# Mixture-of-experts gate: lane tables on POOL, and a running sum along the tiles for the tokens' ranks

## The chip, the core and the metric

The kernel runs on one core of a Trainium2 chip. The core has PE (matrix products, results in PSUM), DVE (elementwise work and reductions), ACT (activation functions), POOL (a second, programmable elementwise engine, which also issues the indirect gathers) and SP, whose queue issues plain transfers. The engines run side by side and wait for each other through semaphores. The metric is the device time of one execution in microseconds. Three timed executions of the kernel before stand beside one profiled execution.

## What is computed

The program is two layers of a graph network over 6250 nodes with 256 features. Each layer has a sum over 100,000 edges and an attention part; the first is followed by a mixture of experts, the second by a feed-forward part on selected nodes. The change lies in the gate of the mixture of experts:

```python
gate_logits = x @ gate_w + gate_b                    # 6250 x 16 experts
topk_vals, topk_idx = jax.lax.top_k(gate_logits, K)  # K = 2
topk_w = jax.nn.softmax(topk_vals, axis=-1)
h = jax.nn.relu(jnp.einsum('bsh,ehf->bsef', x, w1) + b1)
expert_out = jnp.einsum('bsef,efh->bseh', h, w2) + b2
sel = jnp.take_along_axis(expert_out, topk_idx[:, :, :, None], axis=2)
moe = jnp.sum(topk_w[..., None] * sel, axis=2)
```

The kernel computes each expert only for the tokens that chose it. The gate therefore has to give each of the two choices of every token a place: the rank of the token among all tokens of that expert, and a start for the expert.

## The kernel before

Each token is a partition in one of T = 49 tiles of P = 128 tokens. The gate, `gate()` from line 1281, works in C = 7 chunks of CT = 7 tiles. It has no planner; every engine's order is written out by hand, and a `wait_ge` on a counting semaphore stands ahead of whatever needs another's result.

**ACT** per chunk: the root of the variance (`root`, L1380), then per tile the normalisation (`apply`, L1384) and a copy of the transposed tile out of PSUM (`copy_xxt`, L1389).

**PE** per chunk c: first `rank(c - 2)`, then per tile two transposes (`turn`, L1639) and two products with the gate's weights (`gate`, L1647). `rank` counts, for each token of chunk c, the tokens ahead of it that chose the same expert. `taken[:, c, 0:CT, :]` is 1 where a token picked an expert. A strictly triangular matrix `before` counts the partitions ahead within a tile (L1654), six products with `ones` add the earlier tiles of the chunk (L1656, with 96, 80, 64, 48, 32 and 16 columns), and one adds everything up to the chunk's start, held in slot CT of `taken` (L1657). After the last chunk one product sums the experts' totals (`column_ps`, L1672), 24 filler products keep PE busy (`busy`, L1278), and 98 products build the list of slots from tables and masks (L1683).

**DVE** is a software pipeline over the chunks. While chunk c is normalised (`sums` L1419, `moments` L1425, `scales` L1430 and L1432), chunk c - 2 is chosen (`bias`, `best`, `equal`, `weigh`, `first`, `choose`, `leave_out`, the middle four twice, then `take` L1477 and `carry` L1483), chunk c - 3 gets its lanes and windows from the ranks (`own` L1489, `rank` L1494, `to_whole` to `window_number`), and for chunk c - 4 `mark` makes the 14 lane tables (L1524). A table is a row of 128 numbers a token that holds the tile's number at the token's lane and zero elsewhere. `mark` stands in seven pairs among the others. `take` comes ahead of `scales(c)`, `carry` behind it.

Behind the loop, a chain of small instructions turns the totals into the experts' offsets (L1591 to L1608, each `link` waits for itself); between its steps stand the work of the last chunk and the seven pairs of `mark(C - 2)`. Then come seven wide comparisons (`high`, L1612), each followed by a scaling on DVE (L1617) or on ACT (L1403); the 14 tables of the last chunk follow the third of them. POOL has no work in the gate.

Of the kernel before, what the change touches and what calls it, by code (L numbers as in the profile page):

```python
# [247 lines left out]
class Kernel:  # L248
# [1031 lines left out]
    def gate(self):  # L1280
# [10 lines left out]
        with ExitStack() as ctx:  # L1291
# [18 lines left out]
            taken = s.sb("taken", [P, C + 1, CT + 1, E], BF16)  # L1310
            ones = s.sb("ones", [P, P], BF16)
            before = s.sb("before", [P, P], BF16)
            own_rank = s.sb("own_rank", [P, 2, CT, E])
# [36 lines left out]
            CH = 14  # L1350
            PL = 7
            by_act = [c for c in range(C - 1) if c % 2]
# [5 lines left out]
            with nc.Block() as block:  # L1358
                @block.sync
                def _(sp):  # L1360
# [13 lines left out]
                    sp.wait_ge(self.beta_in, 16)  # L1374

# [30 lines left out]
                def _(dve):  # L1406
                    n = [0]

                    def link(ins, j=None):
                        ins.then_inc(chain, 1)  # L1410
                        n[0] += 1
                        if j is not None:
                            mark(C - 2, j)
                        dve.wait_ge(chain, n[0])
# [59 lines left out]
                    def take(c):  # L1474
                        if 0 <= c < C:
                            dve.wait_ge(chosen, CH * c + 12)
                            nc.vector.tensor_tensor(taken[:, c, 0:CT, :], pick[:, c, 0, :, :], pick[:, c, 1, :, :], ALU.add).then_inc(chosen, 1)  # L1477

                    def carry(c):
                        if 0 <= c < C:  # L1480
                            dve.wait_ge(chosen, CH * c + 13)
                            with nc.allow_low_precision(reason="whole numbers up to T"):
                                nc.vector.tensor_reduce(taken[:, c + 1, CT, :], taken[:, c, :, :].rearrange("p t e -> p e t"), AX_X, ALU.add).then_inc(chosen, 1)  # L1483
# [44 lines left out]
                    nc.vector.memset(taken[:, 0, CT, :], 0.0).then_inc(ready, 1)  # L1528
                    nc.vector.memset(self.listed[:, :], 0).then_inc(ready, 1)
                    nc.vector.tensor_copy(ones[:, :], self.ones[:, :]).then_inc(ready, 1)  # L1530
                    nc.vector.tensor_copy(before[:, :], self.before[:, :]).then_inc(ready, 1)
                    for j in range(CT):
# [8 lines left out]
                    dve.wait_ge(ready, 8)  # L1541
# [1349 lines left out]
```

## Time and profile before

| | us |
|---|---|
| timed runs, median (lowest to highest) | 2626.71 (2626.49 to 2627.77) |
| the profiled execution's own time | 2623.84 |
| its span in the trace | 2622.1 |
| gate, first DVE instruction to the experts' first POOL instruction | 1156.55 to 1259.65 |
| six of seven chunks' scales ready | 1216.61 |
| last chunk's totals ready | 1233.78 |
| first wide comparison | 1240.51 |
| last list product | 1255.55 |

Over the whole span PE is busy 86%, DVE 55%, ACT 33% and POOL 61%. The gate is 103 us of it. A line of the time order gives the start, the length, the engine, the line of the kernel, the operation and what it writes and reads; in brackets stands the idle time before it and what ended it. Lengths of neighbours on one engine overlap, so what an instruction costs is the distance to the next start.

### The profile page before, as it was taken

To read this page: it belongs to the slowest core of one execution; us is meant where nothing else is said; L and a number is where in the kernel's file an instruction comes from. 1 tells how busy PE (TensorE), PEld (TensorE's weight loads), DVE (VectorE), ACT (ScalarE), POOL (GpSimd) and SP (SyncE) were. 2 spreads that over 40 slices of the span, in tenths; PEclk is the share of its full clock that TensorE was granted. 3 is DMA by queue.
4 is the path that set the end of the run, shared out by engine and by line. 5 is a ranking of instruction groups with operands and counts; after the bars stand their busy time and mean duration, and the time that the engine had idled before them with its cause. 6 is when DMAs were issued, how large, how long until landed. Compare 5 with 4: busy or idle time off the path is not lost. (4 is left out here: it accounts for less than half of the span.)

```text
span 2622.1 us, 48474 instructions
## 1 busy us (share of the span) xinstructions
PE 2249.8 (86%) x13041; PEld 1893.4 (72%) x13042; DVE 1438.6 (55%) x3979; ACT 859.8 (33%) x2513; POOL 1596.1 (61%) x2187
## 2 busy tenths in 40 slices
PE   7967777788878766668899999999989999995998
PEld 5745555566656544457799999788879999994898
DVE  9865444445544544458322222478867777777111
ACT  2512222222222111135233333366643434331333
POOL 4777777777777777730465555588855555550333
PEclk9988998878887777655999999999999999997999
DMA  5233333333333333332233343232211111111121
GB/s 165 89 111 103 100 102 100 102 102 101 102 102 102 102 102 102 103 121 71 93 108 106 125 140 108 73 103 78 78 57 43 46 43 44 42 46 55 35 36 29
DMA packets 138623, 227.41 MB, mean 87 GB/s; under 512 B 26651, under 2 KB 99056, under 8 KB 138546
## 3 DMA queue, kind: packets, MB, share of 16 engines
q0 software_dynamic: 56240, 142.70, 19.4%
q1 hardware_dynamic: 81186, 82.10, 9.4%
q10 hardware_dynamic: 1120, 1.71, 0.2%
q8 instruction: 34, 0.56, 0.1%
q14 instruction: 43, 0.35, 0.0%
HBM read 175.10 MB, written 51.30 MB: 86 GB/s over the span
## 5 line engine op out<-in xcount | busy, mean ns | idle before, releaser
L945 POOL DMA_INDIRECT all_XN<-h_table,l_srcI x782 | 770.5, 985 | 243.7 <-issue 231.6
L1148 PE MATMUL gcn_acc<-all_XN,gcn_hot 128*128 128x256 f32 x796 | 258.6, 481 | 131.3 <-DMA all_XN<-h_table,l_srcI 118.5
L1148 PE MATMUL gcn_acc<-all_XN 128*128 128x256 f32 x768 | 247.5, 478 | 112.3 <-DMA all_XN<-h_table,l_srcI 98.2
L1148 PEld LDWEIGHTS gcn_acc<-all_XN,gcn_hot 128*128 128x128 f32 x796 | 180.1, 237 | 193.8 <-issue 123.1
L1148 PEld LDWEIGHTS gcn_acc<-all_XN 128*128 128x128 f32 x768 | 172.1, 235 | 170.2 <-issue 98.1
L1839 ACT ACTIVATE moe_hidden<-moe_hid_ps,moe_b 128x128 f32<-128x128 f32 x420 | 131.6, 364 | 281.4 <-PE moe_hid_ps L1920 281.4
L1920 PEld LDWEIGHTS moe_hid_ps<-moe_xst,held_held 128*128 128x128 f32 x1680 | 203.9, 193 | 11.7 <-issue 7.0
L1045 DVE COPY_PREDICATED gcn_last_seen<-gcn_seen_sb,gcn_seen 128x392 f32<-128x392 int32 x98 | 57.7, 588 | 281.3 <-ACT gcn_seen_sb L879 281.3
L879 ACT COPY gcn_seen_sb<-gcn_seen 128x392 f32<-128x392 f32 x98 | 47.6, 486 | 496.9 <-PE gcn_seen L1155 495.0
L1920 PE MATMUL moe_hid_ps<-moe_xst,held_held 128*128 128x128 f32 x1680 | 207.1, 277 | 1.9 <-DVE moe_xst L1860 1.9
L1927 PE MATMUL moe_y_ps<-held_held,moe_hidden 128*128 128x256 f32 x840 | 199.2, 380 | 0.2 <-DVE moe_y L1891 0.2
L2507 PEld LDWEIGHTS att_hid_ps<-att_xpt,held_held 128*128 128x128 f32 x1568 | 184.2, 193 | 3.3 <-ACT att_xpt L2371 0.7
L2507 PE MATMUL att_hid_ps<-att_xpt,held_held 128*128 128x128 f32 x1568 | 184.4, 276 | 0.5 <-ACT att_xpt L2371 0.5
L2515 PE MATMUL att_f_ps<-held_held 128*128 128x256 f32 x784 | 179.5, 382 | 2.4 <-ACT held_held L2381 1.0
L1037 DVE SCALAR_TENSOR_TENSOR all_X<-gcn_acc,all_XN,all_X 128x256 f32 x392 | 170.1, 474 | 13.3 <-PE gcn_acc L1148 13.1
L1927 PEld LDWEIGHTS moe_y_ps<-held_held,moe_hidden 128*128 128x128 f32 x840 | 151.4, 190 | 17.2 <-issue 0.5
L2515 PEld LDWEIGHTS att_f_ps<-held_held 128*128 128x128 f32 x784 | 145.1, 190 | 24.0 <-ACT held_held L2381 6.0
L1756 POOL DMA_INDIRECT moe_ring<-rows_table,moe_row x108 | 105.9, 980 | 84.0 <-POOL moe_row L1754 78.5
L1860 DVE COPY moe_xst<-moe_turned 128x256 f32<-128x256 f32 x106 | 45.0, 424 | 149.4 <-PE moe_turned L1900 149.4
L2048 POOL DMA_INDIRECT held_held<-slots_out,all_slot x98 | 102.3, 1044 | 35.9 <-issue 16.5
L1754 POOL COPY moe_row<-moe_listed 128x1 int32 (+1 forms) x108 | 21.0, 194 | 158.9 <-POOLq L1265 113.3
L2381 ACT ACTIVATE held_held<-att_hid_ps,early_b 128x128 f32<-128x128 f32 x392 | 110.6, 365 | 18.3 <-PE att_hid_ps L2507 18.3
(431 smaller groups left out, 4702.9 us busy)
## 6 DMA issues: line engine op xcount, KB each, us to landing
held_held<-in_e_w SPq DMA_DIRECT2D x32, 512.0 KB, 4.6
slots_out<-moe_y SPq DMA_DIRECT2D x105, 128.0 KB
all_XN<-h_table,l_srcI POOLq DMA_INDIRECT x782, 2.8
all_X<-in_x SPq DMA_DIRECT2D x7, 896.0 KB, 11.0
rows_table<-all_XN SPq DMA_DIRECT2D x7, 896.0 KB, 4.2
z_table<-held_held SPq DMA_DIRECT2D x49, 128.0 KB, 2.0
x_table<-all_XN SPq DMA_DIRECT2D x49, 128.0 KB, 1.7
out<-all_X SPq DMA_DIRECT2D x49, 128.0 KB
```

The lines of the kernel that those rows point to most:

```text
L945: nc.gpsimd.indirect_dma_start(msg[b][:, c, :], None, self.h_table, bass.IndirectOffsetOnAxis(self.srcI[:, GE * g + c:GE * g + c + 1], 0)) ...
L1037: nc.vector.scalar_tensor_tensor(x, acc[b % NA][:, :], scale[:, k, ds(g, 1)], x, ALU.mult, ALU.add).then_inc(added, 1)
L1045: nc.vector.copy_predicated(last_seen[:, :], seen_sb[k % 2][:, :], seen[k % NP][:, :]).then_inc(lasts_kept, 1)
L1148: last = nc.tensor.matmul(acc[b % NA][:, :], hot[b % NH][:, c, :], msg[b][:, c, :], start=(c == 0), stop=(c == n - 1))
L1756: nc.gpsimd.indirect_dma_start(ring[:, k * D:k * D + D], None, self.rows_table, bass.IndirectOffsetOnAxis(row_1[k][:, :], 0)).then_inc(lan ...
L1839: last = nc.scalar.activation(hidden[:, 2 * k + f, :], hid_ps[k][:, f, :], ACT.Relu, bias=b1[:, c:c + 1])
L1920: last = nc.tensor.matmul(hid_ps[k][:, f, :], w1[p][:, q, c:c + P], xst[:, q, :], start=(q == 0), stop=(q == KB - 1))
L1927: last = nc.tensor.matmul(y_ps[:, :], hidden[:, f, :], w2[p][:, f, :], start=(f == 0), stop=(f == FB0 - 1))
L2048: nc.gpsimd.indirect_dma_start(ys[t % 2][:, c, :], None, self.slots_out, bass.IndirectOffsetOnAxis(self.slot[:, t, c:c + 1], 0)).then_inc( ...
L2381: last = nc.scalar.activation(hidden[:, c, :], hid_ps[k][:, f, :], ACT.Relu, bias=b1[:, c:c + 1])
L2507: last = nc.tensor.matmul(hid_ps[k][:, f, :], W1[:, b, c:c + P], xpt[:, b, :], start=(b == 0), stop=(b == KB - 1))
L2515: last = nc.tensor.matmul(f_ps[:, :], hidden[:, f, :], W2[:, f, :], start=(f == 0), stop=(f == FB1 - 1))
```

## The change

In `gate()` the lane tables leave DVE. A new block on POOL waits for the constants, then chunk by chunk for the lanes (`placed`), and makes the 14 tables with the same operation. All seven chunks are one straight run of 98 instructions.

`taken` is replaced by `upto`, laid out by expert with CT + 1 slots each. `take` writes a chunk's picks into slots 1 to CT (now with a stride); `carry` runs one scan along the 128 numbers, with a multiplier `joined` of zero at each expert's slot 0 and one elsewhere, so that slot j holds the count up to tile j - 1 of the chunk. A new step `carry_on` copies slot CT to the next chunk's slot 0. PE's `rank` is then two products: `before` with slots 1 to CT, and `from_here` = 1 - `before` with slots 0 to CT - 1. It waits for the scan (`chosen` at CH * c + 14) where it waited for `take`. Three more constants are made at the start of the gate.

```diff
+                @block.gpsimd
+                def _(pool):
+                    pool.wait_ge(ready, READY)
+                    for c in range(C):
+                        pool.wait_ge(placed, PL * c + 6)
+                        for j in range(CT):
+                            for i in (j, CT + j):
+                                last = nc.gpsimd.tensor_scalar(tables[:, c, i, :], iota_b[:, :], lane[:, c, i:i + 1], float(CT * c + j + 1), ALU.is_equal, ALU.mult)
+                            last.then_inc(mark_ready, 1)
...
-                            nc.vector.tensor_tensor(taken[:, c, 0:CT, :], pick[:, c, 0, :, :], pick[:, c, 1, :, :], ALU.add).then_inc(chosen, 1)
+                            nc.vector.tensor_tensor(upto[:, c, :, 1:CT + 1].rearrange("p e t -> p t e"), pick[:, c, 0, :, :], pick[:, c, 1, :, :], ALU.add).then_inc(chosen, 1)
...
-                                nc.vector.tensor_reduce(taken[:, c + 1, CT, :], taken[:, c, :, :].rearrange("p t e -> p e t"), AX_X, ALU.add).then_inc(chosen, 1)
+                                nc.vector.tensor_tensor_scan(counts, joined[:, :, :].rearrange("p e t -> p (e t)"), counts, 0.0, ALU.mult, ALU.add).then_inc(chosen, 1)
+
+                    def carry_on(c):
+                        if 0 <= c < C - 1:
+                            dve.wait_ge(chosen, CH * c + 14)
+                            nc.vector.tensor_copy(upto[:, c + 1, :, 0:1], upto[:, c, :, CT:CT + 1]).then_inc(chosen, 1)
...
-                    def mark(c, j):
-                        if 0 <= c < C:
-                            dve.wait_ge(placed, PL * c + 6)
-                            for i in range(j, PC, CT):
-                                last = nc.vector.tensor_scalar(tables[:, c, i, :], iota_b[:, :], lane[:, c, i:i + 1], float(CT * c + j + 1), ALU.is_equal, ALU.mult)
-                            last.then_inc(mark_ready, 1)
...
                     def rank(c):
-                        pe.wait_ge(chosen, CH * c + 13)
+                        pe.wait_ge(chosen, CH * c + 14)
                         after(pe, placed, PL * (c - 2) + 1)
                         ranks = rank_ps[c % 2]
-                        nc.tensor.matmul(ranks[:, :, :], before[:, :], taken[:, c, 0:CT, :], start=True, stop=False)
-                        for later in range(1, CT):
-                            nc.tensor.matmul(ranks[:, later:CT, :], ones[:, :], taken[:, c, 0:CT - later, :], start=False, stop=False)
-                        nc.tensor.matmul(ranks[:, :, :], ones[:, :], taken[:, c, CT:CT + 1, :].broadcast_to([P, CT, E]), start=False, stop=True).then_inc(ranked, 1)
+                        nc.tensor.matmul(ranks[:, :, :], before[:, :], upto[:, c, :, 1:CT + 1].rearrange("p e t -> p t e"), start=True, stop=False)
+                        nc.tensor.matmul(ranks[:, :, :], from_here[:, :], upto[:, c, :, 0:CT].rearrange("p e t -> p t e"), start=False, stop=True).then_inc(ranked, 1)
```

PE's order where chunk 2 begins, before (`gate_logit_ps` are the logits, `gate_turned` the transposes, `gate_rank_ps` the ranks):

```order
L1647 MATMUL gate_logit_ps<-gate_gate_w,gate_xxt 128x16 x4
L1654 MATMUL gate_rank_ps<-gate_taken,gate_before 128x112
L1656 MATMUL gate_rank_ps<-gate_taken,gate_ones 128x96
L1656 MATMUL gate_rank_ps<-gate_taken,gate_ones 128x80
L1656 MATMUL gate_rank_ps<-gate_taken,gate_ones 128x64
L1656 MATMUL gate_rank_ps<-gate_taken,gate_ones 128x48
L1656 MATMUL gate_rank_ps<-gate_taken,gate_ones 128x32
L1656 MATMUL gate_rank_ps<-gate_taken,gate_ones 128x16
L1657 MATMUL gate_rank_ps<-gate_taken,gate_ones 128x112
L1639 MATMUL gate_turned<-all_ident,all_XN 128x128 x4
```

and in the changed kernel:

```order
L1651 MATMUL gate_logit_ps<-gate_gate_w,gate_xxt 128x16 x4
L1658 MATMUL gate_rank_ps<-gate_upto,gate_before 128x112
L1659 MATMUL gate_rank_ps<-gate_upto,gate_from_here 128x112
L1643 MATMUL gate_turned<-all_ident,all_XN 128x128 x4
L1651 MATMUL gate_logit_ps<-gate_gate_w,gate_xxt 128x16 x2
```

Eight products have become two, in the same place between the chunks.

DVE's order in the chain of offsets behind the loop, before (`all_XT` written from `gate_iota_b` is a pair of lane tables, `gate_own_rank` to `gate_window` the last chunk's work):

```order
L1591 TENSOR_SCALAR gate_total_i<-gate_column_ps 128x16
L1524 TENSOR_SCALAR all_XT<-gate_iota_b,gate_lane 128x128 x2
L1489 TENSOR_TENSOR gate_own_rank<-gate_pick,gate_rank_ps 128x224
L1593 TENSOR_SCALAR gate_tiles_i<-gate_total_i 128x16
L1524 TENSOR_SCALAR all_XT<-gate_iota_b,gate_lane 128x128 x2
L1494 TENSOR_REDUCE moe_rank_of<-gate_own_rank 128x14
L1595 TENSOR_SCALAR gate_tiles<-gate_tiles_i 128x16
L1524 TENSOR_SCALAR all_XT<-gate_iota_b,gate_lane 128x128 x2
L1499 CAST gate_whole<-moe_rank_of 128x14
L1597 SCALAR_TENSOR_TENSOR gate_tile_end<-gate_tiles,gate_zero 128x16
```

and in the changed kernel:

```order
L1598 TENSOR_SCALAR gate_total_i<-gate_column_ps 128x16
L1506 TENSOR_TENSOR gate_own_rank<-gate_pick,gate_rank_ps 128x224
L1600 TENSOR_SCALAR gate_tiles_i<-gate_total_i 128x16
L1511 TENSOR_REDUCE moe_rank_of<-gate_own_rank 128x14
L1602 TENSOR_SCALAR gate_tiles<-gate_tiles_i 128x16
L1516 CAST gate_whole<-moe_rank_of 128x14
L1604 SCALAR_TENSOR_TENSOR gate_tile_end<-gate_tiles,gate_zero 128x16
```

The pairs of tables are gone from between the links of the chain; the rest keeps its order.

## Rows read from the trace of the kernel before

**Rows 1.** Busy us by engine in 10 us: PE, PEld, DVE, ACT, POOL; then PE clock.

```profile
1200.00:1210.00 10.00, 9.88 (x55) 9.13 (x54) 9.72 (x56) 6.88 (x18) 0.00 (x0) 0.50 0.27 93
```

**Rows 2.** Time order of DVE (start us, us, line): the chunks' scales.

```profile
1178.68 0.17 DVE L1432 SCALAR_TENSOR_TENSOR gate_shift<-gate_mv,gate_rs 128x7 f32<-128x7 f32 x1
...
1187.81 0.17 DVE L1432 SCALAR_TENSOR_TENSOR gate_shift<-gate_mv,gate_rs 128x7 f32<-128x7 f32 x1
...
1216.38 0.20 DVE L1430 RECIPROCAL gate_rs<-gate_sd 128x7 f32<-128x7 f32 x1 [0.21 <-ACT gate_sd L1380]
1216.61 0.17 DVE L1432 SCALAR_TENSOR_TENSOR gate_shift<-gate_mv,gate_rs 128x7 f32<-128x7 f32 x1
```

**Rows 3.** Time order of ACT and PE where a chunk begins.

```profile
1178.88 1.09 ACT L1384 ACTIVATE all_XN<-all_X,gate_shift,gate_rs 128x256 f32<-128x256 f32 x2 [0.47 <-DVE gate_shift L1432]
1178.94 0.29 PEld L1654 LDWEIGHTS gate_rank_ps<-gate_taken,gate_before 128*128 128x128 bf16 x1
...
1179.54 0.29 PEld L1639 LDWEIGHTS gate_turned<-all_ident,all_XN 128*128 128x128 f32 x2
```

**Rows 4.** Groups by line and shape in the gate: count | busy us, mean ns.

```profile
L1524 DVE TENSOR_SCALAR all_XT<-gate_iota_b,gate_lane 128x128 bf16<-128x128 bf16 x98 | 19.5, 246 | 0.0
...
L1597 DVE TENSOR_TENSOR_SCAN gate_tile_end<-gate_tiles,gate_zero 128x16 f32<-128x16 f32 x1 | 0.2, 180 | 0.0
...
L1600 DVE TENSOR_TENSOR gate_tile_start<-gate_tile_end,gate_tiles 128x16 f32<-128x16 f32 x1 | 0.2, 164 | 0.0
```

**Rows 5.** Time order of DVE while the last chunk is chosen.

```profile
1226.90 0.39 DVE L1489 TENSOR_TENSOR gate_own_rank<-gate_pick,gate_rank_ps 128x224 f32<-128x224 bf16 x1 [0.20 <-PE gate_rank_ps L1657]
...
1231.54 0.41 DVE L1524 TENSOR_SCALAR all_XT<-gate_iota_b,gate_lane 128x128 bf16<-128x128 bf16 x2
1231.86 0.27 DVE L1457 TENSOR_TENSOR gate_marked<-gate_marked,gate_early 128x112 f32<-128x112 f32 x1
1232.16 0.27 DVE L1462 TENSOR_REDUCE gate_number<-gate_marked 128x7 f32<-128x112 f32 x1
...
1233.02 0.38 DVE L1483 TENSOR_REDUCE gate_taken<-gate_taken 128x16 bf16<-128x128 bf16 x1
```

**Rows 6.** Time order: the totals' product and DVE's chain of offsets.

```profile
1233.50 0.22 PE L1672 MATMUL gate_column_ps<-gate_taken,gate_ones 128*128 128x16 bf16 x1
...
1233.78 0.17 DVE L1591 TENSOR_SCALAR gate_total_i<-gate_column_ps 128x16 int32<-128x16 f32 x1 [0.26 <-PE gate_column_ps L1672]
...
1237.20 0.96 DVE L1604 TENSOR_TENSOR held_held<-gate_pick,gate_start_b 128x1568 bf16<-128x1568 bf16 x1
...
1240.51 0.99 DVE L1612 TENSOR_TENSOR all_XT<-gate_tile_of,gate_iota 128x1596 bf16<-128x1596 bf16 x1
```

**Rows 7.** Time order: PE's filler, the last chunk's tables, the list's last products.

```profile
1233.57 8.00 PE L1278 MATMUL gate_list_ps<-all_ones 128*128 128x512 bf16 x24
...
1244.67 2.35 DVE L1524 TENSOR_SCALAR all_XT<-gate_iota_b,gate_lane 128x128 bf16<-128x128 bf16 x14
...
1251.14 4.41 PE L1683 MATMUL gate_list_ps<-all_XT 128*128 128x228 bf16 x42
```

**Rows 8.** Single lines on POOL in other stages: ns min/median/max.

```profile
L473 POOL TENSOR_SCALAR front_shift<-front_mv,front_rs x49: 266/470/1764, 31.9 to 123.5; 128x1 f32<-128x1 f32 x49
...
L469 POOL TENSOR_TENSOR front_sd<-front_mv,all_small x49: 179/188/521, 30.6 to 122.6; 128x1 f32<-128x1 f32 x49
...
L2327 POOL COPY att_qs<-all_XT x49: 387/396/430, 1931.7 to 2350.0; 128x256 f32 x42, 128x256 f32<-128x256 f32 x7
...
L2349 POOL TENSOR_TENSOR held_held<-held_held x49: 722/726/730, 1943.6 to 2373.1; 128x256 f32<-128x256 f32 x49
```

**Rows 9.** POOL and DVE side by side in the attention stage; then that DVE line alone.

```profile
1994.20 0.72 POOL L2349 TENSOR_TENSOR held_held<-held_held 128x256 f32<-128x256 f32 x1 [2.44 <-DVE held_held L2426]
1994.25 0.82 DVE L2451 TENSOR_SCALAR all_XN<-all_X,att_ln_c_mv,att_ln_c_rs  x1
...
L2451 DVE TENSOR_SCALAR all_XN<-all_X,att_ln_c_mv,att_ln_c_rs x49: 411/822/830, 1958.3 to 2388.0; - x42, 128x256 f32<-128x256 f32 x7
```

More of the change, by code:

```diff
@@ L1309, in gate @@
             pick = s.sb("pick", [P, C, 2, CT, E], BF16)
-            taken = s.sb("taken", [P, C + 1, CT + 1, E], BF16)
+            upto = s.sb("upto", [P, C, E, CT + 1], BF16)
+            joined = s.sb("joined", [P, E, CT + 1], BF16)
             ones = s.sb("ones", [P, P], BF16)
             before = s.sb("before", [P, P], BF16)
+            from_here = s.sb("from_here", [P, P], BF16)
             own_rank = s.sb("own_rank", [P, 2, CT, E])
@@ L1349, in gate @@
              placed, gap_ready, gap_exp, chain, mark_ready, high_ready, high_by_act, high_by_dve, high_used, rows_out) = [s.sem(n) for n in names.split()]
-            CH = 14
+            CH = 15
             PL = 7
+            READY = 11
             by_act = [c for c in range(C - 1) if c % 2]
@@ L1407, in _, with link @@
                     n = [0]
-                    def link(ins, j=None):
+                    def link(ins):
                         ins.then_inc(chain, 1)
                         n[0] += 1
-                        if j is not None:
-                            mark(C - 2, j)
                         dve.wait_ge(chain, n[0])
@@ L1518, in window_number @@
                             nc.vector.tensor_copy(window[:, c, :], window_i[:, :]).then_inc(placed, 1)
-                    def mark(c, j):
-                        if 0 <= c < C:
-                            dve.wait_ge(placed, PL * c + 6)
-                            for i in range(j, PC, CT):
-                                last = nc.vector.tensor_scalar(tables[:, c, i, :], iota_b[:, :], lane[:, c, i:i + 1], float(CT * c + j + 1), ALU.is_equal, ALU.mult)
-                            last.then_inc(mark_ready, 1)
                     nc.vector.memset(zero[:, :], 0.0).then_inc(ready, 1)
-                    nc.vector.memset(taken[:, 0, CT, :], 0.0).then_inc(ready, 1)
+                    nc.vector.memset(upto[:, 0, :, 0:1], 0.0).then_inc(ready, 1)
+                    nc.vector.memset(joined[:, :, 0:1], 0.0).then_inc(ready, 1)
+                    nc.vector.memset(joined[:, :, 1:CT + 1], 1.0).then_inc(ready, 1)
                     nc.vector.memset(self.listed[:, :], 0).then_inc(ready, 1)
@@ L1531, in _ @@
                     nc.vector.tensor_copy(before[:, :], self.before[:, :]).then_inc(ready, 1)
+                    nc.vector.tensor_scalar(from_here[:, :], self.before[:, :], -1.0, 1.0, ALU.mult, ALU.add).then_inc(ready, 1)
                     for j in range(CT):
@@ L1540, in _ @@
                     nc.vector.tensor_copy(iota_2[:, :, :], iota[:, 0:MAX_TILES].unsqueeze(2).broadcast_to([P, MAX_TILES, 2])).then_inc(ready, 1)
-                    dve.wait_ge(ready, 8)
+                    dve.wait_ge(ready, READY)
                     for c in range(1, C + 2):
-                        f, g, m = c - 2, c - 3, c - 4
+                        f, g = c - 2, c - 3
                         sums(c, 0)
@@ L1587, in _ @@
                         carry(f)
+                        carry_on(f)
                     c = C - 1
@@ L1617, in _ @@
                             nc.vector.tensor_scalar(h[:, :, 1, :], h[:, :, 0, :], self.place_no, None, ALU.mult).then_inc(high_by_dve, 1)
-                        if c == 2:
-                            for j in range(CT):
-                                mark(C - 1, j)
                     nc.vector.tensor_copy(self.span[:, 0:E, 0], tile_start[0:1, :])
@@ L1670, in _ @@
                     rank(C - 1)
-                    pe.wait_ge(chosen, CH * C)
-                    nc.tensor.matmul(column_ps[:, 0:E], ones[:, :], taken[:, C, CT, :], start=True, stop=True).then_inc(counted, 1)
+                    pe.wait_ge(chosen, CH * C - 1)
+                    nc.tensor.matmul(column_ps[:, 0:E], ones[:, :], upto[:, C - 1, :, CT], start=True, stop=True).then_inc(counted, 1)
                     self.busy(list_bank, 24)
```

24 lines of the change are left out of this document (9 added, 15 removed).

## The prediction, made before the changed kernel had run

> **What bounds the kernel now.** I read the summary of the page first: the span is 2622.1 us, and the profiled execution itself took 2623.84 us against a median of 2626.71 us for the three timed runs. Differences that I work out in the trace are therefore taken off 2623.84 and carried over unchanged to the median, 2.87 us higher. The change touches only the gate, 1156.5 to 1259.6 us of the span, in which nothing of another stage runs; the experts start behind a barrier, so what the gate's end moves, the end of the program moves.
>
> Inside the gate the busy times come first [rows 1]: PE 9.88 and DVE 9.72 us of 10 with POOL at zero, at a granted clock of 0.50 (1.2 GHz). Two engines are full, so the order in time has to say which one holds the other. The DVE timeline gives the period of one chunk as the distance of two `shift` instructions [rows 2]: 9.13 us from 1178.68 to 1187.81, while DVE makes no tables yet, and 28.80 us for the three periods from 1187.81 to 1216.61, in which each holds 14 tables. In the early periods PE and ACT set the pace. In the later ones DVE does: its `reciprocal` then waits only 0.21 us for ACT's root. So DVE costs 28.80 - 3 x 9.13 = 1.41 us there. After the last chunk of logits DVE is alone on the path: choosing chunk 6, from 1226.4 us on [rows 5], the chain of offsets [rows 6], the wide masks for the list [rows 7].
>
> **DVE loses the tables.** There are 98 of them, mean 246 ns [rows 4], but on the path a pair costs what the next instruction starts later: 1231.54 to 1231.86, 0.32 us [rows 5]. Four places, at first as if POOL disturbed nothing:
> - The loop: seven pairs are 2.3 us, so DVE's period falls from 9.5 to 7.2 us, and PE and ACT set 9.13 again. Gain 1.4 us.
> - Choosing chunk 6, up to 1233.02 [rows 5]: seven pairs, 2.27 us. Some of it comes back, since instructions that follow their own input directly start 0.30 us apart (1231.86 to 1232.16), while a table, which waits for nothing, costs only 0.16. In the first half other work still fills such waits; about 0.2 us returns. DVE's `own` for chunk 5, at 1226.90, waited 0.20 us for eight products and now waits for two, some 0.2 us less. Gain 2.3 us.
> - The offsets, 1233.78 to 1240.51, 6.73 us [rows 6]: the seven pairs go, but each instruction of the chain now waits for the one ahead. Walking the order with 0.18 us behind a small instruction that is waited for (the subtraction took 164 ns [rows 4]), 0.30 behind `own` and `rank`, and an estimated half of 0.18 where nothing waits gives 2.1 us up to the wide multiplication (3.42 before, 1233.78 to 1237.20); the multiplication, the reduction and the addition take 3.1 of the 3.3 us. Gain 1.5 us.
> - The masks: 14 tables stood in the middle, 1244.67 to 1246.94, and all behind them shifts. Gain 2.3 us. What is late next? PE's filler products take 8.00 us from 1233.57, and 98 list products at 4.41 / 42 = 0.105 us are 10.3 us [rows 7]; the column product stands 5.5 us before the masks after the change, so PE can't end before 8.0 + 10.3 - 5.5 = 12.8 us behind the first mask. DVE's way is 15.0 - 2.3 = 12.8 us too. The gain holds, and nothing beyond it.
>
> **The scan.** The scan of 16 elements took 180 ns, the subtraction of as many 164 ns [rows 4]: one more nanosecond an element, so 128 elements are some 0.41 us, against 0.38 for the reduction that it replaces. `take` now writes with a stride; at most 0.05 us. Behind the scan `carry_on` waits for it, 0.2 us more a chunk. All of it hides in the slack of DVE's period (7.5 of 9.13 us). What is queued behind the new wait is more serious: PE's rank products waited for `take`, which came before the scales, and now wait for the scan, behind which all of PE's next chunk stands. In the early period PE loaded the first rank product at 1178.94 and the next transpose at 1179.54, while ACT's first normalised tile was there at 1178.88 + 0.60 = 1179.48 [rows 3] (the row holds two tiles, 1.09 us). With the scan ending at 1179.18 and two products of 112 columns (0.19 us at 1.2 GHz, where eight took about 0.45) PE is ready at 1179.45: a tie, 0 us, with 0.1 a period if the scan is held up. Once, behind chunk 6, it costs: scan 0.41 and two products before the column, where the column came at 1233.50, 0.48 us after the reduction's start [rows 5, 6]; about 0.2 us lost. Start-up: three more small instructions ahead of the first statistics, 0.3 us lost. PE's six products fewer bring nothing else.
>
> Sum so far: 1.4 + 2.3 + 1.5 + 2.3 - 0.2 - 0.3 = 7.0 us.
>
> **POOL's tables, and what they do to DVE.** No row shows this instruction on POOL at 128 elements. Its one-element form with a per-partition scalar and two operations took at least 266 ns; a copy of 256 elements 396 ns and an addition of two 256-element tensors 726 ns against 188 ns for one element, thus 0.8 to 2.1 ns an element [rows 8]. That is 0.37 to 0.53 us a table, 0.80 if each of the two operations costs an addition's pass. One tensor comes in, as with the copy, so I take 0.40: 14 are 5.6 us of a period of 9.13. POOL keeps up, beginning near 1183 us, since chunk 0's lanes are done about halfway through the period that starts at 1178.68.
>
> But the two engines hold each other up. Beside POOL's addition (1994.20, 0.72 us) a DVE instruction on 256 elements took 0.82 us, where its least is 0.411 [rows 9]. It began 0.05 us later, so it was held until 0.46 us after POOL's start: not to the end, but to about 0.26 us before it, the fixed part of a POOL instruction. For a table of 0.40 us that leaves a hold of 0.14 us, rarely met in full: 0.03 us a DVE instruction on average, 0.07 with a table of 0.53. I take 0.06. Affected are instructions with two inputs in SBUF and plain copies and scalings, 16 a chunk in the loop, 13 while chunk 6 is chosen, 13 in the offsets. Costs: the loop 16 x 0.06 = 1.0 us, within the slack, but 0.1 us on `shift` or the scan in some four periods, 0.3 us; choosing 0.8; offsets 0.8; and beside the masks some eight tables of chunk 6 are left, each slipping in between two wide DVE instructions for its hold of 0.14, 1.1 us. Together 3.0 us. Net gain 7.0 - 3.0 = 4.0 us: 2623.84 - 4.0 = 2619.8 for the profiled execution, **2622.7 us** for the median.
>
> The Trainium skill speaks against the change here: SBUF — State Buffer, section "Who interferes with whom", says that a DVE instruction with two SBUF inputs or in a two-port mode and a reading GpSimd instruction exclude each other for the whole instruction. The rows above show DVE going on before POOL's end is recorded, so the trace agrees with the exclusion and not with its full length. By the full length the sum is the second rival's. GPSIMD Engine Reference, section "Engine selection", calls one-input work on GpSimd about line-rate, which by its text is the 0.37 us end.
>
> **The rivals.**
> 1. *No hold to speak of.* The small instructions mostly miss POOL's reads. Then 6 to 7 us are gained: 2619.7 to 2620.7. For it: the hold is short in [rows 9]. Against: 42 instructions on the path and wide masks that can't miss.
> 2. *A table holds DVE for its whole length.* A DVE instruction then waits half of 0.38 us, 0.19. The period is 7.5 + 16 x 0.19 = 10.5 us, 31.5 for three, 2.7 worse than 28.80; choosing 2.3 - 2.5, offsets 1.5 - 2.5, masks 2.3 - 8 x 0.37; with scan and start-up 5.1 us lost: 2631.8. It turns to a loss where the mean wait passes 0.11 us. The held row speaks against it.
> 3. *POOL becomes the bound, slower.* Tables run from 1183, and the last must be there by about 1250 for PE's last 14 list products: 67 / 98 = 0.68 us a table, DVE's holds on POOL included. At 0.80 us they end at 1261.6, and the list 1.5 us later, 7.5 us after the 1255.6 of now: 2634.2. For it: an untried form, and a longest of 1764 ns for one element where POOL itself was held [rows 8]. Against: the price per element that it needs.
> 4. *The change does not do what it says*: nothing stands in POOL's queue in the gate, and the order shows the 98 tables there and none on DVE. I give it nothing.
>
> **How the numbers follow.** Forecast 0.50, rival 1 0.28, rival 2 0.10, rival 3 0.12. A measurement tells 0.2%, 5.3 us, from no change. Rival 1 is faster by that, and so is the upper edge of the forecast (a hold near 0.03 us, or a warmer clock earlier in the filler): 0.36. Rival 3 is slower, and a small part of rival 2: 0.14. The rest, 0.50, is the same. The range leaves out the far ends: from 2619.0 to 2632.0.
>
> **What the profile of the changed kernel would show.** The `shift` instructions 9.1 to 9.2 us apart in all periods (right); 9.8 or more is rival 2. POOL's tables at 0.37 to 0.5 us and DVE's two-input rows within 0.1 us of their lengths now. The rank products start 0.5 us after `shift`, and the transposes within 0.1 us of them. The column product near 1230.5, the first mask near 1237.5, the list read near 1252. A list product waiting for POOL is rival 3. A clock other than 0.50 in the loop would overturn the period.

## The result, and the profile of the changed kernel

The changed kernel took 2638.49 us (median of five runs, 2635.24 to 2640.72) where the kernel before took 2627.77 (five runs, 2626.49 to 2629.56): a ratio of 1.0039 with a 95% interval of [1.0028, 1.0050]. It is slower by 10.7 us. The prediction was 4 us faster, with a range that ended at 2632.0. The profiled execution took 2638.52 us, its span 2636.8 us.

The gate begins 4.5 us later in this profile (its first DVE instruction at 1161.07 us against 1156.55), because stages that the change does not touch took longer. So the gates are compared from that first instruction, and "+" times below count from it. The mark at the other end of the gate is the instruction of DVE that reads the finished list: it stood at +99.5 us before and stands at +112.9 now. From there to the end of the span it was 1366.1 us before and is 1362.8 now; in ten of the twelve profiles below it lies between 1360 and 1365. The gate alone lost 13.4 us. So the 14.7 us between the two profiled executions are 4.5 ahead of the gate, 13.4 in it and 3.3 back behind it; what moves outside the gate is not explained by any row, and the gate's length is the surer measure of the change than the medians' 10.7 us.

First the order in time of DVE in the changed kernel (start us, us, line): where it waits for ACT's root, where a chunk's scales are made, the choice of the last chunk, the offsets, the first wide mask, and the read of the list.

```profile
1201.69 0.20 DVE L1441 RECIPROCAL gate_rs<-gate_sd 128x7 f32<-128x7 f32 x1 [1.26 <-ACT gate_sd L1393]
1201.93 0.17 DVE L1443 SCALAR_TENSOR_TENSOR gate_shift<-gate_mv,gate_rs 128x7 f32<-128x7 f32 x1
...
1229.99 0.27 DVE L1453 TENSOR_TENSOR gate_logits<-gate_logit_ps,gate_gate_b 128x112 f32<-128x112 f32 x1 [3.21 <-PE gate_logit_ps L1651]
...
1234.40 0.65 DVE L1488 TENSOR_TENSOR gate_upto<-gate_pick 128x112 bf16<-128x112 bf16 x1
1235.09 0.42 DVE L1495 TENSOR_TENSOR_SCAN gate_upto<-gate_joined,gate_upto 128x128 bf16<-128x128 bf16 x1
...
1236.20 0.17 DVE L1598 TENSOR_SCALAR gate_total_i<-gate_column_ps 128x16 int32<-128x16 f32 x1 [0.59 <-PE gate_column_ps L1674]
...
1241.79 1.04 DVE L1619 TENSOR_TENSOR all_XT<-gate_tile_of,gate_iota 128x1596 bf16<-128x1596 bf16 x1
...
1273.97 0.28 DVE L1631 TENSOR_SCALAR gate_xxt<-gate_list_ps 128x114 f32<-128x114 f32 x1 [22.31 <-PE gate_list_ps L1685]
```

DVE gained what it should: `reciprocal` now waits 1.23 to 1.26 us for ACT in each of the three late periods (0.21 in [rows 2]), so the loop is paced by PE and ACT. The first mask stands at +80.7, where it stood at +84.0 [rows 6]. At the end DVE sits idle for 22.31 us. The waits of the gate name who it waits for, and what stands behind that (engine, line waited for: us in total, times, longest):

```profile
POOL all_XT L1386 <- DVE gate_lane L1530: 36.8, 1, 36.8
DVE gate_xxt L1631 <- PE gate_list_ps L1685: 22.3, 1, 22.3
...
PE gate_list_ps L1685 <- issue: 16.0, 3, 8.3
```

DVE waits for PE, and PE waits for "issue", which is time in which the profile shows nothing that it waited for. POOL waited once, for the first chunk's lanes, and never again: from then on it always had work behind it. The busy time by engine in 10 us (PE, PEld, DVE, ACT, POOL, then the granted TensorE clock) says the same, beside [rows 1]:

```profile
1200.00:1210.00 10.00, 10.00 (x50) 9.24 (x51) 8.23 (x39) 6.57 (x16) 8.99 (x13) 0.50 0.29 103
...
1240.00:1250.00 10.00, 8.60 (x67) 6.11 (x66) 9.82 (x12) 3.73 (x3) 10.00 (x8) 1.00 0.01 2
1250.00:1260.00 10.00, 2.25 (x21) 1.66 (x18) 1.56 (x7) 1.15 (x1) 9.82 (x14) 0.85 0.00 0
1260.00:1270.00 10.00, 2.82 (x14) 1.88 (x14) 0.00 (x0) 0.00 (x0) 9.82 (x15) 0.67 0.00 0
```

From 1252.8 us on POOL works alone, but for PE's two short bursts. PE's order in time shows the list being fed chunk by chunk; the last three groups of 14 products wait until POOL has made their chunk's 14 tables. The last tables of these chunks end at 1251.14, 1261.04 and 1270.94 us, each 0.10 us before PE goes on:

```profile
1249.08 1.58 PE L1685 MATMUL gate_list_ps<-held_held,all_XT 128*128 128x228 bf16 x14
1251.24 1.58 PE L1685 MATMUL gate_list_ps<-all_XT 128*128 128x228 bf16 x14 [0.57 <-issue]
1261.14 2.82 PE L1685 MATMUL gate_list_ps<-all_XT 128*128 128x228 bf16 x14 [8.32 <-issue]
1271.04 2.82 PE L1685 MATMUL gate_list_ps<-all_XT 128*128 128x228 bf16 x14 [7.09 <-issue]
```

And the lines that answer to [rows 4] (ns shortest/median/longest, first and last start):

```profile
L1386 POOL TENSOR_SCALAR all_XT<-gate_iota_b,gate_lane x98: 704/715/2538, 1188.1 to 1270.2; 128x128 bf16<-128x128 bf16 x98
...
L1488 DVE TENSOR_TENSOR gate_upto<-gate_pick x7: 653/657/781, 1180.1 to 1234.4; 128x112 bf16<-128x112 bf16 x7
...
L1495 DVE TENSOR_TENSOR_SCAN gate_upto<-gate_joined,gate_upto x7: 410/416/425, 1183.6 to 1235.1; 128x128 bf16<-128x128 bf16 x7
```

A table on POOL takes 715 ns, where DVE took 246. The pace of 14 tables is the length of the window from one chunk's first table to the next one's (us, POOL busy, clock, DMA share, GB/s): chunks 1, 4 and 5.

```profile
1199.24:1210.67 11.43, 10.29 (x15) 0.50 0.31 111
...
1233.62:1251.22 17.60, 17.02 (x14) 0.82 0.01 1
1251.22:1261.01 9.79, 9.69 (x14) 0.80 0.00 0
```

In the loop the tables of one chunk take 11.1 to 11.5 us, about 0.8 each, in a period of 9.13: POOL falls 2.0 to 2.4 us behind with every chunk. Chunk 4's, beside DVE's offsets and masks, take 17.6 us. Once the other engines are done a table costs 0.70 us; why it costs 0.1 us more in the loop, also where DVE is idle, is open. All 98 take 82.8 us. Without the 6.2 us that chunk 4 took beyond a chunk of the loop, the list would by estimate still come 7 us later than before (13.4 - 6.2): the price carries about half of the loss, and what DVE does to POOL the other.

### The profile page after: what moved, and what is told of

It is laid out like the page before. It is cut to its first block and busy times, and to the rows that moved or that the text cites. A ratio compares the mean times of both kernels' runs of the same rounds, so it can differ in the third digit from the quotient of the medians.

```text
span 2636.8 us, 48400 instructions
## 1 busy us (share of the span) xinstructions
PE 2248.1 (85%) x12999; PEld 1890.2 (72%) x13000; DVE 1428.9 (54%) x3890; ACT 857.8 (33%) x2513; POOL 1674.2 (63%) x2285
## 5 line engine op out<-in xcount | busy, mean ns | idle before, releaser
L1148 PE MATMUL gcn_acc<-all_XN 128*128 128x256 f32 x768 | 239.9, 467 | 124.1 <-DMA all_XN<-h_table,l_srcI 110.0
L1148 PEld LDWEIGHTS gcn_acc<-all_XN 128*128 128x128 f32 x768 | 166.7, 228 | 178.3 <-issue 101.1
L1893 DVE TENSOR_TENSOR moe_y<-moe_y_ps,moe_b 128x256 f32<-128x256 f32 x105 | 44.5, 424 | 128.0 <-PE moe_y_ps L1929 103.7
## 6 DMA issues: line engine op xcount, KB each, us to landing
all_X<-in_x SPq DMA_DIRECT2D x7, 896.0 KB, 11.1
```

Of the source, the lines that this page charges most:

```text
L1148: last = nc.tensor.matmul(acc[b % NA][:, :], hot[b % NH][:, c, :], msg[b][:, c, :], start=(c == 0), stop=(c == n - 1))
```

## The experiments

The theory from the profile: POOL's price of a table is above what its queue can bear, and this backlog is the whole loss of the gate. The rivals: the running sum costs (its `take` is three times as long as before), or POOL working beside DVE costs wherever it runs. The kernels ran on four other chips, slower than the first (the kernel before took 2774 to 2779 us there), so each ratio is to the kernel before on its own chip; the kernel before was profiled on the first chip only. Whether its gate may be compared across chips is tested below, with the changed kernel.

**The running sum without POOL.** All tables go back to DVE, in their old places; the sum by the scan stays.

```diff
-                        for j in range(CT):              # POOL: all seven pairs
+                        for j in range(BY_DVE[c], CT):   # BY_DVE = [7, 7, 7, 7, 7, 7, 7]
```

> The ranks by the running sum, as in the changed kernel, but all 98 tables back on DVE at their old places and none on POOL. Theory A (POOL's tables, 0.80 us each in the changed kernel's trace, 98 in one queue from 27 us behind the gate's start, are the whole loss; the list waits for them): the loss goes. What stays is the rank part alone: DVE sets the period while it makes tables, and take is 0.44 us longer there (657 against 216 ns), the scan and carry_on 0.2: three periods and the last chunk, 2 to 3 us slower than before. Rival B (the running sum, with PE's rank products behind the scan, is what costs): 8 us or more slower than before.

2775.40 us, ratio 1.0004 [0.9986, 1.0022]; the gate takes 100.9 us, 1.5 more than before. The periods in which DVE makes tables are 9.84 us here (9.60 before, 28.80 / 3 [rows 2]). So the running sum by itself costs the gate 1.5 us: less than the 2 to 3 expected, and no cause of 13.4. In the time it can't be seen.

**POOL's tables without the running sum.** The kernel before, with its eight rank products, and the tables made by POOL.

```diff
+                @block.gpsimd
+                def _(pool):
+                    ... (the changed kernel's block)
                     def mark(c, j):
-                        if 0 <= c < C:
+                        if False:
```

> The kernel before with eight rank products and the reduction, and only the tables moved to POOL. Theory A: as slow as the changed kernel within 1 us, about 10 to 11 us slower than before; the last list product ends when POOL's 98th table does, about 83 us behind the first. Rival B: near the kernel before, within 2 us.

2786.17 us, ratio 1.0039 [1.0023, 1.0054], the same ratio as the whole change; gate 112.1 us, 12.6 more than before. Its POOL line:

```profile
L1383 POOL TENSOR_SCALAR all_XT<-gate_iota_b,gate_lane x98: 704/715/2541, 1336.5 to 1418.1; 128x128 bf16<-128x128 bf16 x98
```

The loss comes with the tables on POOL, whatever makes the ranks.

**Five chunks by POOL, two by DVE.** The changed kernel with `BY_DVE = [0, 0, 0, 0, 0, 7, 7]`: the tables of chunks 5 and 6 are DVE's again.

> The changed kernel with POOL making the 70 tables of chunks 0 to 4 and DVE those of chunks 5 and 6 at their old places behind the loop. Theory A: 70 tables at 0.78 us end 55 us behind the first, 82 us behind the gate's start, when the list begins, so that PE never waits for POOL; gained against before are 1.3 us in the loop and some of choosing chunk 6, lost are 0.4 us at the start and 0.4 in take: 1 to 2.5 us faster than before. Rival C (POOL's reads hold DVE up wherever the two run together, and that is a good part of the loss): most of the contention is still there, so still 3 us or more slower than before.

2768.38 us, ratio 0.9971 [0.9954, 0.9988]: faster than the kernel before. The gate takes 97.5 us. POOL's 70 tables last 59.6 us, 4.6 more than expected (the last one 2.54 us, beside the masks), and PE begins the list when DVE's first mask is scaled, not when POOL is done:

```profile
1393.51 1.58 PE L1707 MATMUL gate_list_ps<-all_XT 128*128 128x228 bf16 x14 [1.45 <-DVE all_XT L1642]
```

The same instruction, 28 times fewer, turns the sign. POOL beside DVE is thus not what costs the gate its time; being last is. The time fell by 8 us, though, and the gate by only 1.9; the 1 to 2.5 us expected are met by the gate alone.

**What POOL charges for.** After the first chunk POOL makes three tables in each of eight forms; DVE makes its addition of 112 elements in six layouts.

```diff
+   nc.gpsimd.tensor_scalar(tried[...], iota_b, lane, float(i + 1), ALU.is_equal, ALU.mult)   # as is, L1392
+   nc.gpsimd.tensor_scalar(tried[...], iota_b, lane, None, ALU.is_equal)                     # L1396
+   nc.gpsimd.tensor_scalar(tried[...], iota_b, lane, float(i + 1), ALU.mult, ALU.mult)       # L1398
+   nc.gpsimd.tensor_copy(tried[...], iota_b)                                                 # L1402
+   ... (64 columns, L1404; 4-byte in and out, L1406; DVE's additions, L1633 to L1638)
```

> As the first of this list, with instructions added that nothing uses: on POOL three each of eight forms (the table as it is; from the 4-byte iota; the comparison alone; two multiplications in place of comparison and multiplication; one multiplication by a constant; a copy; the table at 64 columns; 4-byte in and out), and on DVE, in its idle time behind the last chunk but one, six additions of 112 numbers with the output laid out in different ways. Theory A1 (each of two operations costs a pass over the elements): one operation and a copy are near 0.38 us, all forms with two near 0.70, the half table near 0.48. Rival A2 (the comparison is the slow one): two multiplications near 0.40, the comparison alone near 0.6. Rival A3 (2-byte numbers are slow on POOL): the 4-byte forms near 0.40 and the 2-byte copy near 0.6. DVE: outputs of 2-byte numbers 16 bytes apart take 0.65 us as take does; if the distance matters through partial words, 4 bytes and 18 bytes apart cost the same and 4-byte numbers at 32 bytes do not; if it is the 16 bytes, 18 bytes apart is fast. With the output in order and the input strided instead: 0.25 us or less if only the write matters.

```profile
L1392 POOL TENSOR_SCALAR all_XT<-gate_iota_b,gate_lane x3: 706/789/829, 1336.8 to 1338.4; 128x128 bf16<-128x128 bf16 x3
...
L1396 POOL TENSOR_SCALAR all_XT<-gate_iota_b,gate_lane x3: 590/591/597, 1341.2 to 1342.3; 128x128 bf16<-128x128 bf16 x3
L1398 POOL TENSOR_SCALAR all_XT<-gate_iota_b,gate_lane x3: 361/362/367, 1342.9 to 1343.6; 128x128 bf16<-128x128 bf16 x3
...
L1402 POOL COPY all_XT<-gate_iota_b x3: 279/280/283, 1345.4 to 1345.9; 128x128 bf16<-128x128 bf16 x3
L1404 POOL TENSOR_SCALAR all_XT<-gate_iota_b,gate_lane x3: 495/500/606, 1346.2 to 1347.2; 128x64 bf16<-128x64 bf16 x3
...
L1633 DVE TENSOR_TENSOR all_XT<-gate_pick x1: 211/211/211, 1380.1 to 1380.1; 128x112 bf16<-128x112 bf16 x1
L1634 DVE TENSOR_TENSOR all_XT<-gate_pick x1: 650/650/650, 1380.3 to 1380.3; 128x112 bf16<-128x112 bf16 x1
L1635 DVE TENSOR_TENSOR all_XT<-gate_pick x1: 889/889/889, 1380.5 to 1380.5; 128x112 bf16<-128x112 bf16 x1
```

It is the comparison (rival A2). Two multiplications, the same operands and sizes, take 362 ns; the comparison alone takes 591, with the multiplication behind it 704. Reading and writing 4-byte numbers changes little (809 ns median, 709 at least). Half the columns take 495 instead of 706: (706 - 495) / 64 = 3.3 ns an element, and some 0.28 us that do not depend on the length. On DVE the addition with its output in one piece takes 211 ns; with the outputs 16 bytes apart, as the changed `take` writes, 650; 18 bytes apart 889. Written in order and read with a stride it took 497 (4-byte outputs 32 bytes apart 345, 2-byte outputs 4 bytes apart 298), so reading with a stride costs too: 0.25 us or less was expected if only the write mattered. The three instructions of a form stand one behind the other and the kernel ran once, so this tells of prices only, and of the layouts by one instruction each. The comparison is not the whole rule either: one multiplication by a constant took 517 ns, more than the two with a per-partition scalar.

**The cheap form in the changed kernel.** The forecast's price, about 0.36 to 0.40 us a table, put in the place of 0.71. The list comes out wrong, and one DVE instruction behind it keeps it within the tokens.

```diff
-  nc.gpsimd.tensor_scalar(tables[:, c, i, :], iota_b[:, :], lane[:, c, i:i + 1], float(CT * c + j + 1), ALU.is_equal, ALU.mult)
+  nc.gpsimd.tensor_scalar(tables[:, c, i, :], iota_b[:, :], lane[:, c, i:i + 1], 1.0 / 128, ALU.mult, ALU.mult)
```

> The changed kernel with POOL's tables made by two multiplications in place of a comparison and a multiplication; the comparison is left out, so the tables hold other numbers, and one more DVE instruction of about 0.28 us keeps the list within the tokens. It puts the price of the forecast (0.36 to 0.40 us a table) in the place of the measured 0.71 and leaves all else. Theory A (the price is the step that failed): 98 tables at 0.36 to 0.45 us keep up with the lanes, the last is made within 2 us of its lane, the list waits for nothing on POOL, the gate takes 95 to 96.5 us and the time is 3 to 5 us below the kernel before, where the prediction put it. Theory B (even with cheap tables POOL and DVE hold each other up): gate 98 us or more, chunk periods over 9.5 us.

```profile
L1386 POOL TENSOR_SCALAR all_XT<-gate_iota_b,gate_lane x98: 368/374/1916, 1331.0 to 1391.5; 128x128 bf16<-128x128 bf16 x98
...
  DVE gate_lane L1530: 55.2, 6
```

The last line is POOL's waits for lanes (us, times). The gate takes 94.4 us, 5.1 under the kernel before. POOL waits for lanes six times, the first chunk's among them: it keeps up with the loop. The chunk periods are 9.12 to 9.33 us. Only the last chunk's tables come late, 10.5 us behind its lanes and not 2, since beside the masks two of them take 1.92 us; they still end 2.5 us before the last mask. So the step that failed is the price, and with the price of the forecast the gate would have gained even more than forecast. The time, however, was 2780.71, ratio 1.0010 [0.9991, 1.0029]: the expected 3 to 5 us are not there. They go behind the gate: from the list to the end it is 1373.7 us, against 1360.1 in the first kernel of the next paragraph. In the 300 us after the list PE is busy 284.9 us here and 293.0 there, and DVE waits 42.1 us against 19.1 for its writes of the experts' results. The wrong list sends other rows to the experts; that this is the reason is argued, not tried. The gate of this kernel says something, its time does not.

**The tables divided.** Two kernels: DVE makes 17 of the 49 pairs, most of them where it has slack, POOL the other 64 tables; the first has the running sum (with `take` written in order), the second the old eight products.

```diff
+            BY_DVE = [2, 2, 2, 7, 0, 0, 4]
-                        for j in range(CT):
+                        for j in range(BY_DVE[c], CT):
```

> The changed kernel with the tables divided: DVE makes 2, 2, 2, 7, 0, 0, 4 of the seven pairs of chunks 0 to 6 (17 pairs, 34 tables), POOL the other 64, and take writes its output in order and reads its inputs with a stride. Theory A (POOL's price of 0.71 us a table is the whole of the loss): 64 tables need 46 us, POOL is done before the list wants its last ones, the list never waits for POOL, and the gate from its first instruction to the read of the list takes about 95.5 us, 4 us under the kernel before and 17 under the changed one; the time is 3 to 5 us below the kernel before. take falls from 0.65 to about 0.50 us. Theory B (POOL working beside DVE costs in itself, whatever its backlog): the gate stays at 98 us or more though the list waits for nothing on POOL. Theory C (the experts or the half clock in the list cost, not the gate): the gate is 95 to 96 us but the program is no faster than before.

> The kernel before with only the tables divided as in e4_split: its eight rank products, reduction and four-deep sum stay. With e4_split it tells what the running sum is worth once POOL is no longer the bound. Theory A (the running sum costs about 1.5 us in the gate, as e1_sum_only measured it): this gate is 1 to 1.5 us shorter than e4_split's, 94 to 95 us, and the time is 4 to 6 us below the kernel before. Rival D (the running sum pays when DVE has slack, its longer take and scan being hidden and six products a chunk gone from PE): this gate is as long as e4_split's or up to 0.5 us longer.

With the running sum: 2767.97 us, ratio 0.9955 [0.9937, 0.9973], gate 97.6 us. With the old products: 2764.63 us, ratio 0.9947 [0.9930, 0.9965], gate 97.0. `take` fell from 657 to 361 ns, further than the 0.50 expected. Both gates are 2 to 3 us longer than expected, for the same reason: the list still waits for POOL, 2.42 us in the first and 2.79 in the second, since the few tables that POOL makes beside the wide masks are long (the next paragraph). The total count stands at +75.0 and +74.0: the running sum costs 1 us up to there, and 0.6 at the list. Theory A of the second expectation gets the direction, not the size; the two times are not told apart.

**Six chunks by POOL, the last by DVE.** The changed kernel with `BY_DVE = [0, 0, 0, 0, 0, 0, 7]`.

> The changed kernel with the tables of chunk 6 alone made by DVE, as the kernel before makes them; POOL makes the 84 of chunks 0 to 5. By the backlog alone: 84 x 0.78 = 65.5 us from 27 us behind the gate's start, so POOL ends at 92.7 us, and chunk 5's last list products follow there; DVE pays for seven pairs (2.3 us) in the masks. Theory A: gate 96.5 to 98 us, time 1.5 to 3 us below the kernel before. Theory B (POOL holds DVE up wherever it runs): gate 99 us or more.

2786.86 us, ratio 1.0023 [1.0006, 1.0040], gate 106.0 us: a miss by 8 us for theory A, on the same side as the forecast's. The number is theory B's, its reason is not: DVE is not held up, its periods are 9.12 to 9.25 us and its masks 974 to 983 ns behind the first. It is POOL that is held. The 84 tables took 73.2 us and not 65.5. In the loop POOL makes one in 0.8 us; beside the masks it hardly moves. POOL and DVE in the changed kernel, at the same time:

```profile
1243.56 2.54 POOL L1386 TENSOR_SCALAR all_XT<-gate_iota_b,gate_lane 128x128 bf16<-128x128 bf16 x1
1246.08 2.54 POOL L1386 TENSOR_SCALAR all_XT<-gate_iota_b,gate_lane 128x128 bf16<-128x128 bf16 x1
```

```profile
1242.86 0.69 DVE L1624 TENSOR_SCALAR all_XT<-all_XT,all_small 128x1596 bf16<-128x1596 bf16 x1
1243.47 1.87 DVE L1619 TENSOR_TENSOR all_XT<-gate_tile_of,gate_iota 128x1596 bf16<-128x1596 bf16 x2
1245.38 0.69 DVE L1624 TENSOR_SCALAR all_XT<-all_XT,all_small 128x1596 bf16<-128x1596 bf16 x1
1245.99 0.97 DVE L1619 TENSOR_TENSOR held_held<-gate_tile_of,gate_iota 128x1596 bf16<-128x1596 bf16 x1
```

One table lasts as long as DVE's two masks and a scaling: it starts as one scaling ends (1242.86 + 0.69 = 1243.55) and ends with the next (1245.38 + 0.69 = 1246.07 against 1246.10). POOL gets one table done in each 2.5 us of masks, and DVE's masks are no longer for it: 982 ns median, the first alone 1040 against 991. The Trainium skill (SBUF — State Buffer, section "Who interferes with whom") says that a DVE instruction with two SBUF inputs and a reading GpSimd instruction exclude each other for a whole instruction; these rows agree with it as to POOL, which waits, but not as to DVE: no mask behind the first is held for a table of 0.7 us in return. How the table gets through is not shown: 1.78 us behind the two masks (1243.56 to 1245.34) and its own 0.71 beside the scaling would add up to about the 2.54, and so would being let in at the seams between DVE's instructions.

**The division moved.** The second divided kernel, with DVE making six pairs of the last chunk (`[2, 2, 2, 7, 0, 0, 6]`), and with three pairs of chunk 5 and all seven of chunk 6 (`[2, 2, 2, 7, 0, 3, 7]`); and the changed kernel itself on the same chip.

> e6_split_old with six instead of four pairs of chunk 6 made by DVE, so POOL makes 60 tables instead of 64. In e6_split_old POOL made 34 tables after chunk 3 and the list waited 2.8 us for the last of them. Theory A (the rest of that gate's loss is POOL's last tables, each 0.78 us and up to 2.5 beside the wide masks): POOL is done 3 us or more earlier, DVE's masks end 0.6 us later, the list waits for POOL by 0.5 us at most, and the gate takes 95 to 95.7 us against 97.1. Theory B (the list is already at DVE's pace and the wait only shows slack): 97 to 98 us.

> The same with DVE making three pairs of chunk 5 in the chain of offsets and all seven of chunk 6, so POOL makes 52 tables. Theory A: POOL is done before the masks are half through and no longer matters; DVE pays 0.3 us for the seventh pair and 0.5 to 1 us for three pairs in the chain, so the gate is 0.3 to 1 us longer than e9_retuned's, 95.5 to 96.5 us. Theory B (POOL beside the masks slows DVE): it is shorter than e9_retuned's by 0.5 us or more, because no POOL table is left there.

> The changed kernel itself on this chip, beside the two above. If the backlog on POOL is all there is, the gate takes 112 to 113 us as in the first profile, POOL's 98 tables take 82 to 84 us, and the ratio to the kernel before is 1.003 to 1.005 here too. If something of the first chip decided, the gate differs by over 1 us.

2762.55 us, ratio 0.9935 [0.9912, 0.9959], gate 94.8 us; 2769.90, ratio 0.9976 [0.9960, 0.9993], gate 95.3; the changed kernel 2786.95, ratio 1.0034 [1.0016, 1.0053], gate 112.9. PE's last products of the list in the first of them:

```profile
1400.07 1.58 PE L1696 MATMUL gate_list_ps<-all_XT 128*128 128x228 bf16 x14
1401.82 3.07 PE L1696 MATMUL gate_list_ps<-all_XT 128*128 128x228 bf16 x28 [0.17 <-issue]
```

Two pairs fewer on POOL took the wait from 2.79 to 0.17 us and the gate from 97.0 to 94.8. With no POOL table left beside the masks, but for the end of one, it is 0.4 us longer, not shorter, so POOL does not slow DVE there either: theory A in both, each gate 0.2 us under the range given for it. The changed kernel's gate is the same to 0.1 us on both chips (112.9), which is why the 99.5 us of the kernel before are used for the other chips too.

**The best once more.**

> e9_retuned once more, because its ratio of 0.9935 is some 18 us where its gate is only 4.7 us shorter than the kernel before, while e10_retuned_more, whose gate differs by 0.5 us, gave 0.9976. Theory A (only the gate differs; what a ratio says beyond it is a spread that the interval of one call does not hold): the gate takes 94.5 to 95.2 us again and the ratio is 0.995 to 0.999. Theory B (the shorter gate brings more behind it, in the experts): the ratio is 0.9935 again within 0.001, and the time from the list to the end is shorter than the 1362 us of the other kernels.

2766.69 us, ratio 0.9966 [0.9948, 0.9985]; gate 94.8 us again, from the list to the end 1361.1. Theory A. The gate explains 4.7 of 2774 us, 0.17%; both ratios are further from 1 than that, the first clearly. The other divided kernels show the same: their gates are 1.8 and 2.4 us shorter than before, their times by the ratio 12 and 15 us. So these ratios can't price the gate, and why the times fall further is open. This kernel is faster than the kernel before on both chips, and than the changed one on the chip where that ran beside it.

## Why the prediction was wrong, point by point

**What bounds the kernel now, and where DVE's tables cost: right.** The periods are 9.12 to 9.25 us as said, and the loop gained 1.30 us (forecast 1.4, with 0.3 of contention taken off). From the last chunk's logits to the total count it is 6.2 us instead of 7.4, a gain of 1.15 (forecast net 1.3). The offsets took 5.6 instead of 6.7, a gain of 1.14 (forecast net 0.7). The masks, from the first to the last scaling, lost 2.2 us with their 14 tables (forecast net 1.2). Start-up cost 0.35 (forecast 0.3). Together 1.30 + 1.15 + 1.14 + 2.2 - 0.35 = 5.4 us; the cheap form shows 5.1 at the list. Without POOL's disturbance 7.0 were forecast and 3.0 taken off for it; 1.6 are missing, 0.4 of them in `take`. So the 4.0 would have been too low even with the forecast's price.

**The scan: right; `take`: wrong.** The scan took 416 ns (0.41). `take` "with a stride; at most 0.05 us" took 657 ns, 0.44 more than its 216. Only its share after chunk 6 lies on the path. It was estimated from nothing: no row showed a 2-byte output with a stride, and the bound should have said so.

**What POOL does to DVE: the mechanism there, the victim wrong.** 3.0 us were charged to DVE. Its rows hardly moved: `shift` 167 ns at the median and 293 at the longest, the small casts and subtractions 20 to 30 ns more on average and up to 0.13 us at times, the wide masks 982 ns as before. It was POOL that waited, up to 2.54 us for one table, and what DVE does to POOL stood in no term of the sum. [rows 9] showed DVE held behind POOL's addition; I carried that direction over to instructions of another length and another order of issue.

**POOL's price: this is the step that failed.** "One tensor comes in, as with the copy, so I take 0.40." Measured: 715 ns, one in about 0.8 us in the loop, above the turning point of 0.68 that the third rival had worked out. The bounds of 0.37 to 0.53, and 0.80, held the value. The choice between them went by the number of inputs, while here the operation decides (704 ns against 362, with the same inputs), and none of [rows 8] has a comparison. The cheap form shows that this choice alone decided the sign of the gate's change. The Trainium skill (GPSIMD Engine Reference, section "Engine selection") calls one-input work roughly line-rate; here the one-input comparison took 3.3 ns an element beyond its fixed part and nearly three times DVE's 246 ns, so the page and the measurement differ for it.

**The third rival: right in kind, short in size.** It gave 7.5 us later for 0.80 us a table; the list came 13.4 us later. In its own terms: POOL's last table would end at 1266.4 us on the old clock (109.8 us behind the gate's start) instead of 1261.6, since 98 tables took 82.8 us, 0.845 each, with DVE's hold on POOL beside the masks in them, some 6 us. That is 4.8 us. The last 14 products then took 2.82 and not 1.5 us: 1.3. Its chance of 0.12 was too small, since its condition (0.68) lay inside the bounds of an operation that no row showed.

## What to carry to other kernels

When work moves to an engine that has not done this operation in the trace, the price is that of the operation, not of an instruction with as many inputs; if the turning point lies inside the bounds, no sum behind it is worth more than that bound, and three instructions of it in a spare corner of the kernel settle it. An idle engine is best given the part of the work that its real pace can finish in time: here 60 of 98 tables, with the others where DVE has slack. A queue that falls behind is not caught up evenly: ask what runs beside its last entries.

## What the runs showed of the hardware that was not expected

- POOL, 128 elements of 2 bytes: copy 280 ns, two multiplications 362, one multiplication by a constant 517, comparison 591, comparison and multiplication 704. One operation with a constant is dearer than two with a per-partition scalar; why is open. Tables of 0.71 us begin 0.79 us apart or more in the loop and 0.70 us apart when the other engines are idle; why is open too.
- DVE, addition of 112 elements of 2 bytes: 211 ns in one piece, 298 with outputs 4 bytes apart, 650 at 16 bytes, 889 at 18; as 4-byte numbers 32 bytes apart 345. The same addition, written in order from inputs read with a stride, took 497 ns in the trial and 361 in the gate.
- PE after idling: at a granted clock of 1.00 (2.4 GHz) 14 list products took 1.58 us; after waits of 8.32 and 7.09 us the clock was 0.52 and 0.50 (1.2 GHz) while they ran, and they took 2.82. In the divided kernels, after waits of 2.42 and 2.79 us, they took 1.87 at a mean clock of 0.80 and 1.58 at 1.00. A PE that waits long for POOL is then also slow.
